# Three mixture-of-experts stages: rows stored in token order and gathered by slot tile, with the order of some instructions changed in two attention stages

## Chip, core and metric

The kernel runs on one core of a Trainium2 chip. Its time is the device time of one execution in microseconds (us); the median of three runs of the kernel before is 4051.39 us (4050.05 to 4054.77).

## What is computed

The reference carries x of shape (128, 32, 128), 4096 tokens of 128 channels in float32, through twelve sublayers: four times cross-attention (to 257 context tokens, or, in the second, causal over the first 32), a self-attention or a retention, and a feed-forward stage. Each reads a layernorm of x and is added to it. Cut to the three mixtures and the two kinds of stage that the change touches:

```python
# L0 ffn: mixture, top 2 of 8 experts, plus a shared expert (a_moe)
probs = softmax(normed @ router_w.T); top_v, top_i = top_k(probs, 2); gates = softmax(top_v)
out = sum_e comb[:, e] * swiglu(normed, gate_up_w[e], down_w[e]) + swiglu(normed, shared...)
# L1 ffn: mixture, top 2 of 8, gelu, at most 1280 tokens for an expert (c_moe)
# L3 ffn: rmsnorm, top 1 of 8, u1 * sigmoid(u2), biases (u_moe)
# L0 attn: six layers of linear attention and a leaky feed-forward part (the stage "l")
# L0, L2, L3 xattn: att = softmax(q k / sqrt(8)); y = (att v) Wo, 16 heads, 257 keys
```

## The kernel before, in words

x lies in on-chip memory as X[128 partitions, 32 tiles, 128 channels], a tile being 128 tokens; four tiles are a chunk, and there are eight chunks. Stages follow one another as blocks. In a block every engine (TensorE, VectorE, ScalarE, GpSimd, SyncE) has its own instruction stream in an order written out by hand; they meet in semaphores alone. In what follows, a stage's name is the prefix of its tiles in the profile: a_cross, l, a_moe, c_self, c_moe, e_cross, retention, q_ffn, t_cross, t_self, t_mlp, u_self, u_moe.

**The mixtures** (`routed_experts`, line 1345) have a head and a loop over slot tiles. In the head VectorE takes the statistics of the chunks (`statistics`, L1736), GpSimd makes factor and shift of each chunk out of small operations with the power function (`deviation`, L1458), ScalarE normalises (`apply`, L1649), TensorE transposes the rows and multiplies them by the router (`turn`, `choose`, L1517 and L1525). The tokens are taken in two halves, g = 0 and 1. For each, VectorE picks the experts (`choose`, L1751), TensorE counts tokens of each expert with two triangular or all-one matrices (L1544), and VectorE works out for each token the slot in which it belongs (`places`, L1772), and for each slot tile the expert that owns it (owner). A slot tile is 128 slots of one expert; a half has 39 slot tiles with two experts for each token (K = 2, in a_moe and c_moe) and 24 with one (K = 1, u_moe), each in 13 or 8 triples. Then GpSimd scatters: `put(g)` (L1482) issues an indirect DMA for each token tile and k, 32 or 16 for a half, which writes 128 normalised rows to their slots in DRAM (L1491). Only when the scatter of a half is complete may SyncE load its triples (`load`, L1427, L1433). Because a slot that no token fills is still computed on, the stage l writes zeros over the slots once: GpSimd sets `blank` and SyncE issues six DMAs of it (L2889). In c_moe VectorE also ranks the tokens of each expert before the loop, to drop those over the capacity (L1814 to L1834).

**The loop over slot tiles** has 78 steps (48 with K = 1). TensorE transposes the tile (`turn_x`, L1587), multiplies it by the owner's first matrix (`up`), transposes the hidden layer (`turn_hidden`), multiplies by the second (`down`); ScalarE and VectorE carry results on; SyncE stores a triple of results back into the slots (L1439). Beside it GpSimd scatters the second half (`put(1)`), and then gathers results: `take(g)` (L1494, L1502), 32 or 16 indirect DMAs for a half, each adding to a tile of X when VectorE combines it (`combine`, L1899, from step 45 on, or 30 with K = 1).

**The stage l** (`linear_transformer`, line 2780) runs 48 chunk steps (six layers of eight chunks) as a software pipeline: in one step TensorE works on chunk `now`, on the attention of the one before (`one`), and on the feed-forward part of the ones before that (`two`, `three`). Its order (L3070 to L3112) puts four bursts of small 32x32 products (`attend`, L3035, 16 products each, one for each tile of the chunk) between the large products `up(two, 2)`, `down(two, 0)` and `up(two, 3)`. GpSimd's order (L2940 to L2954) is: deviation, bias, queries' softmax, deviation and `apply1` for the following chunk, `units` (L2930), and last `leaky(two, 2)` and `leaky(two, 3)` (L2936), for which TensorE's `down(three, 2)` and `down(three, 3)` wait in the next step. ScalarE's `raw(two, 2)` comes ahead of the copy that carries the attention on (L3169 to L3172).

**The cross-attentions** (`cross_attention`; three stages of 128 steps, a batch each): TensorE makes `scores` (L2309) in four banks, VectorE takes the negated maxima in two halves of two banks (`maximum`, L2497), then adds the bias to the next batch's keys (`keys`, L2511), ScalarE takes four exponentials (L2454), the first two after the first half, the others after the second. TensorE's `turn(n - 2, 1)` (L2367) waits for `keys`, since both use the same bank, then come `values` (L2377) and the next `scores`, which also wait for all four exponentials.

## Time and profile before

| what | value |
|---|---|
| median of three runs | 4051.39 us |
| profiled execution, its own time | 4054.11 us |
| its span on the core | 4052.3 us |
| busy of the span: TensorE, VectorE, ScalarE, GpSimd | 85%, 65%, 57%, 61% |
| instructions | 120030 |
| mean granted TensorE clock | 0.92 of full speed |

How to read it: the span runs from the first to the last instruction; what the execution's own time has beyond it lies around the kernel. Busy shares are averages over stages with different limits, so a stage is read by itself: its window, then its timeline. Times in a row are microseconds from the span's start, then the duration; PE is TensorE, PEld its weight load, DVE VectorE, ACT ScalarE, POOL GpSimd. A bracket at a row's end is the idle time before it and what ended it.

### The profile page before, as it was taken

The numbers are of one execution on the slowest core, as the hardware profiler recorded it, in microseconds if no ns is written. First come the engines' busy times: TensorE is split into PE (matmuls) and PEld (weight loads), VectorE is DVE, ScalarE is ACT, GpSimd is POOL, SyncE is SP. The second block draws the span as 40 slices with busy tenths as digits, with TensorE's granted clock in tenths as the row PEclk, the third lists the DMA queues.
The fourth block names the chain that finished last, engine by engine and source line by source line (L and its number), as shares of the span: only waits on it lengthen the run. The fifth ranks groups of instructions, "written<-read, shape, count | busy, mean of one in ns | idle before, by whom it ended". The sixth has DMA issues, their size and how long they took to land. (4 is left out here: it accounts for less than half of the span.)

```text
span 4052.3 us, 120030 instructions
## 1 busy us (share of the span) xinstructions
PE 3461.1 (85%) x44674; PEld 2487.3 (61%) x44674; DVE 2627.4 (65%) x6958; ACT 2325.4 (57%) x6315; POOL 2470.0 (61%) x2844
## 2 busy tenths in 40 slices
PE   8999959999999669698498999978589999786866
PEld 6777737777777447455366777755367777453444
DVE  6777756666666423476434888767767777754655
ACT  6777736666566334287123777755567777544633
POOL 6676656666666543476424887756466766745633
PEclk9999979999999779899699999989599999887978
DMA  2111110000000122201122111110011110000023
GB/s 74 41 35 41 30 69 5 7 11 11 6 7 2 54 63 77 56 17 45 49 72 67 48 47 43 36 65 4 1 47 41 35 41 30 3 2 6 2 91 93
DMA packets 90550, 149.06 MB, mean 37 GB/s; under 512 B 10112, under 2 KB 66816, under 8 KB 89664
## 3 DMA queue, kind: packets, MB, share of 16 engines
q1 hardware_dynamic: 79936, 122.87, 9.8%
q0 software_dynamic: 10240, 20.99, 1.7%
q8 instruction: 261, 4.28, 0.4%
q14 instruction: 113, 0.93, 0.1%
HBM read 112.76 MB, written 31.06 MB: 35 GB/s over the span
## 5 line engine op out<-in xcount | busy, mean ns | idle before, releaser
L2228 POOL TENSOR_TENSOR t_cross_E<-t_cross_E,t_cross_inverse 128x1028 f32<-128x1028 f32 x128 | 243.2, 1900 | 139.7 <-DVE t_cross_inverse L2507 139.7
L2228 POOL TENSOR_TENSOR a_cross_E<-a_cross_E,a_cross_inverse 128x1028 f32<-128x1028 f32 x128 | 243.2, 1900 | 131.9 <-DVE a_cross_inverse L2507 131.9
L2454 ACT ACTIVATE t_cross_E<-t_cross_psum,t_cross_negtop 128x257 f32<-128x257 f32 x512 | 235.9, 474 | 134.6 <-DVE t_cross_negtop L2497 134.6
L2454 ACT ACTIVATE a_cross_E<-a_cross_psum,a_cross_negtop 128x257 f32<-128x257 f32 x512 | 236.0, 474 | 125.8 <-DVE a_cross_negtop L2497 125.8
L2454 ACT ACTIVATE e_cross_E<-e_cross_psum,e_cross_negtop 128x257 f32<-128x257 f32 x512 | 235.9, 474 | 124.2 <-DVE e_cross_negtop L2497 124.2
L2228 POOL TENSOR_TENSOR e_cross_E<-e_cross_E,e_cross_inverse 128x1028 f32<-128x1028 f32 x128 | 243.1, 1899 | 92.7 <-DVE e_cross_inverse L2507 92.7
L3065 PE MATMUL l_psum<-l_ffn_w,l_hidden 128*128 128x128 f32 x1536 | 219.5, 287 | 12.9 <-POOL l_hidden L2938 9.8
L3065 PEld LDWEIGHTS l_psum<-l_ffn_w,l_hidden 128*128 128x128 f32 x1536 | 192.1, 193 | 50.3 <-POOL l_hidden L2938 24.0
L3058 PE MATMUL l_psum<-l_hT,l_ffn_w 128*128 128x512 f32 x384 | 204.3, 635 | 0.9 <-ACT l_hT L3122 0.9
L2497 DVE TENSOR_REDUCE t_cross_negtop<-t_cross_psum 128x2 f32<-128x514 f32 x256 | 165.1, 687 | 47.7 <-PE t_cross_psum L2314 45.9
L2497 DVE TENSOR_REDUCE a_cross_negtop<-a_cross_psum 128x2 f32<-128x514 f32 x256 | 165.1, 686 | 40.3 <-PE a_cross_psum L2309 37.8
L2497 DVE TENSOR_REDUCE e_cross_negtop<-e_cross_psum 128x2 f32<-128x514 f32 x256 | 165.1, 687 | 36.9 <-PE e_cross_psum L2309 32.6
L2367 PE MATMUL a_cross_psum<-const_sb,a_cross_E 128*128 128x128 f32 x1024 | 161.1, 280 | 14.2 <-DVE a_cross_kT L2511 11.5
L2367 PE MATMUL e_cross_psum<-const_sb,e_cross_E 128*128 128x128 f32 x1024 | 160.5, 280 | 14.3 <-DVE e_cross_kT L2511 11.6
L2367 PE MATMUL t_cross_psum<-const_sb,t_cross_E 128*128 128x128 f32 x1024 | 160.9, 280 | 13.5 <-DVE t_cross_kT L2511 11.6
L2917 POOL TENSOR_SCALAR l_normed<-inner,l_moments,l_rstd 128x128 f32<-128x128 f32 x192 | 149.8, 793 | 14.8 <-POOL l_rstd L2911 14.8
L2928 POOL TENSOR_TENSOR l_q<-l_q,l_q_stat 128x512 f32<-128x512 f32 x48 | 50.8, 1058 | 173.0 <-DVE l_q_stat L3201 173.0
L3221 DVE TENSOR_TENSOR inner<-l_psum,inner 128x512 f32<-128x512 f32 x48 | 33.2, 692 | 184.6 <-PE l_psum L3050 184.6
L3042 PEld LDWEIGHTS l_psum<-l_qT,l_ctx 32*32 32x32 f32 x6144 | 65.6, 107 | 114.1 <-issue 108.5
L2367 PEld LDWEIGHTS a_cross_psum<-const_sb,a_cross_E 128*128 128x128 f32 x1024 | 114.8, 142 | 32.9 <-DVE a_cross_kT L2511 30.6
L2367 PEld LDWEIGHTS e_cross_psum<-const_sb,e_cross_E 128*128 128x128 f32 x1024 | 114.1, 141 | 33.1 <-DVE e_cross_kT L2511 31.0
L2938 POOL TENSOR_TENSOR l_hidden<-l_hidden,l_less 128x512 f32<-128x512 f32 x96 | 123.0, 1302 | 18.3 <-ACT l_hidden L3146 18.3
(754 smaller groups left out, 11137.2 us busy)
## 6 DMA issues: line engine op xcount, KB each, us to landing
a_cross_context<-context SPq DMA_DIRECT2D x32, 578.0 KB, 3.7
e_cross_context<-context SPq DMA_DIRECT2D x32, 578.0 KB, 3.7
t_cross_context<-context SPq DMA_DIRECT2D x32, 578.0 KB, 3.7
u_moe_weights<-pack_u_moe SPq DMA_DIRECT2D x1, 5633.0 KB, 16.7
slots<-l_blank SPq DMA_DIRECT2D x6, 832.0 KB, 12.0
a_moe_x_slots<-slots SPq DMA_DIRECT2D x26, 192.0 KB, 2.8
slots<-a_moe_y_slots SPq DMA_DIRECT2D x26, 192.0 KB, 2.0
c_moe_x_slots<-slots SPq DMA_DIRECT2D x26, 192.0 KB, 2.9
```

What stands on the lines that cost most here:

```text
L2228: pool.tensor_tensor(E[:, n % N], E[:, n % N], spread(inverse[:, n % 4], SK, 2), ALU.mult).then_inc(s_unit, 1)
L2367: last = pe.transpose(psum[:, (T_BANK, K_BANK)[c], g * P:(g + 1) * P], E[:, n % N, g, c * P:(c + 1) * P], ident)
L2454: act.activation(E[:, n % N, g], psum[:, g, 0:SK], ACT.Exp, bias=negtop[:, n % 2, g:g + 1], accum_out=total[:, n % 2, g:g + 1]).then_inc(s ...
L2497: dve.tensor_reduce(negtop[:, n % 2, at], psum[:, at, 0:SK], AX.X, ALU.max, negate=True).then_inc(s_top, 1)
L2917: last = pool.tensor_scalar(Y1[:, t], c.tile(t), moments[:, 0, t, 0:1], rstd[:, 0, 1, t:t + 1], ALU.subtract, ALU.mult)
L2928: pool.tensor_tensor(groups, groups, spread(q_stat[:, 2], DH, 2), ALU.mult).then_inc(s_soft, 1)
L2938: pool.tensor_tensor(hidden[:, f], hidden[:, f], less[:, f - 2], ALU.add).then_inc(s_late, 1)
L3042: last = pe.matmul(psum[rows, C_BANK, b * S:(b + 1) * S], ctx[rows, b], qT[rows, b * S:(b + 1) * S], start=True, stop=True)
L3058: pe.matmul(psum[:, U_BANKS[f % 2]], c.ffn(f * P), hT2[:], start=True, stop=True).then_inc(s_up, 1)
L3065: last = pe.matmul(psum[:, D_BANK, t * P:(t + 1) * P], hidden[:, f, t * P:(t + 1) * P], c.ffn((NF + f) * P), start=(f == 0 and t == 0), st ...
L3221: dve.tensor_tensor(c.chunk(), tiles(psum[:, C_BANK]), c.chunk(), ALU.add).then_inc(s_mid, 1)
```

## The change

1. Mixtures. Normalised rows are stored by SyncE in token order in DRAM (`rows`), eight plain DMAs. `place` (slot of a token) is split into slot tile and spot in it. For each pair m of token tile and k, VectorE or GpSimd makes a 128x128 matrix that holds the token's number where its spot is, and TensorE multiplies it by the one-hot matrix of the token's slot tile; the sum over the 32 (or 16) pairs is, for each slot, the number of its token. GpSimd then gathers each slot tile (x_slots) by one indirect DMA with 128 of these numbers. The scatter, `put` and the plain loads are gone, and with them the blanks in l. Results are gathered as before, but in the loop by turns with the slot tiles' gathers.
2. Heads of the mixtures. The norm's factor comes from a square root on ScalarE and a reciprocal on VectorE instead of GpSimd; VectorE applies it to chunks 1 and 3; all statistics come ahead of the first choice.
3. c_moe. The ranking is cut into 18 parts, one at every second step of the loop, from step 2 to step 36.
4. l. TensorE's four bursts `attend` stand together; GpSimd's two `leaky` stand ahead of `units`; ScalarE's `raw(two, 2)` stands behind the copy of the attention.
5. Cross-attentions. VectorE's `keys` stand between the two halves of `maximum`.

```diff
@@ routed_experts, SyncE @@
-            def load(j):
-                g, at = divmod(j, TRIPLES)
-                if at == 0:
-                    sp.wait_ge(s_put[g], puts + 16 * HALF * K)
...
+            def store_rows(c):
...
+                sp.dma_start(slots.rows[c * CHUNK:(c + 1) * CHUNK].rearrange("(t p) d -> p t d", p=P),
+                             rows[:, c * TPC:(c + 1) * TPC]).then_inc(s_rows[c // PART], 16)
@@ GpSimd @@
-            for c in range(PART + 2):
-                deviation(c)
-            put(0)
-            put(1)
+            def index(g):
+                h = of(g)
+                pool.wait_ge(s_spot, g + 1)
+                for n, m in enumerate(BY_POOL):
...
+                    pool.tensor_scalar(at_spot_pool[:, (g * len(BY_POOL) + n) % POOL_RING], core.const("count"), spot[:, k, at:at + 1],
+                                       core.const("token")[:, at:at + 1], ALU.is_equal, ALU.mult).then_inc(s_at_spot_pool, 1)
+            def load(i):
+                j, n = divmod(i, 3)
+                g, at = divmod(i, NS)
+                if at == 0:
+                    pool.wait_ge(s_token, g + 1)
...
+                if n == 0 and j >= 4:
+                    pool.wait_ge(s_x_turn, j - 3)
+                pool.indirect_dma_start(x_slots[:, j % 4, n], None, slots.rows,
+                                        bass.IndirectOffsetOnAxis(ap=token[:, g, at:at + 1], axis=0)).then_inc(s_load[j % 4], 16)
...
+            for g in range(2):
+                index(g)
+            for i in range(NS + AHEAD):
+                load(i)
+            stores_done(pool, TRIPLES)
+            for i in range(NS + AHEAD, COUNT):
+                if i - NS - AHEAD < PAIRS:
+                    take(i - NS - AHEAD)
+                load(i)
@@ TensorE @@
+            def find(g):
+                pe.wait_ge(s_in_tile, g + 1)
+                for m in range(PAIRS):
...
+                    pe.matmul(psum[:, COUNT_BANK + g, FOUND], mine, in_tile[:, k, t], start=m == 0, stop=m == PAIRS - 1).then_inc(s_found, 1)
...
+                if g == 1:
+                    find(0)
                 pe.wait_ge(s_mask, g + 1)
...
+            find(1)
@@ ScalarE @@
+                    act.activation(root[:, at], first, ACT.Sqrt, bias=core.const(eps)[:, 0:1]).then_inc(s_root, 1)
@@ VectorE @@
+                link(dve.tensor_scalar(tile_no[:, 0:K, h], place[:, 0:K, h], 1.0 / P, 0.5 / P - 0.5, ALU.mult, ALU.add))
...
+                dve.tensor_tensor(in_tile[:], spread(tile_no[:, 0:K, h], NS, 3),
+                                  spread(spread(core.const("count")[:, 0:NS], HALF, 1), K, 1), ALU.is_equal).then_inc(s_in_tile, 1)
...
+            def index(g):
+                dve.wait_ge(s_spot, g + 1)
+                for n, m in enumerate(BY_DVE):
...
+                    if n >= RING:
+                        dve.wait_ge(s_found, g * PAIRS + BY_DVE[n - RING] + 1)
+                    dve.tensor_scalar(at_spot[:, n % RING], core.const("count"), spot[:, k, at:at + 1],
+                                      core.const("token")[:, at:at + 1], ALU.is_equal, ALU.mult).then_inc(s_at_spot, 1)
+                dve.wait_ge(s_found, (g + 1) * PAIRS)
+                dve.tensor_copy(token[:, g], psum[:, COUNT_BANK + g, FOUND]).then_inc(s_token, 1)
...
+            for g in range(2):
+                choose(g)
+                places(g)
+                index(g)
@@ loop of VectorE @@
+                if choice == "capacity" and 2 <= i < 38 and i % 2 == 0:
+                    rank((i - 2) // 18, (i - 2) // 2 % 9)
@@ cross_attention, VectorE @@
                 if exists(i, n):
-                    maximum(i, n)
+                    maximum(i, n, 0)
                 if exists(i, n + 1):
                     keys(i, n + 1)
+                if exists(i, n):
+                    maximum(i, n, 1)
@@ linear_transformer, GpSimd @@
-                if now.exists:
-                    units(now)
                 if two.exists:
                     leaky(two, 2)
                     leaky(two, 3)
+                if now.exists:
+                    units(now)
@@ linear_transformer, TensorE @@
                 if one.exists:
-                    attend(one, 0)
+                    for t in range(TPC):
+                        attend(one, t)
                 if two.exists:
                     up(two, 2)
-                if one.exists:
-                    attend(one, 1)
-                if two.exists:
                     down(two, 0)
-                if one.exists:
-                    attend(one, 2)
-                if two.exists:
                     up(two, 3)
-                if one.exists:
-                    attend(one, 3)
-                if two.exists:
                     down(two, 1)
```

Of the pairs m, every fifth (m = 4, 9, ...) is made by GpSimd in a ring of four matrices, the others by VectorE in a ring of eight; a matrix may be overwritten once its product is done.

## Rows read from the trace of the kernel before

**Rows 1.** Stretches: length, then busy time of PE, PEld, DVE, ACT, POOL, granted clock, DMA share, GB/s
```profile
545.00:1373.00 828.00, 790.39 (x11616) 587.23 (x11616) 535.83 (x1586) 479.64 (x816) 544.24 (x625) 0.98 0.02 6
1373.00:1462.00 89.00, 23.70 (x105) 22.08 (x106) 31.74 (x146) 19.46 (x43) 58.35 (x104) 0.51 0.22 84
1462.00:1657.00 195.00, 190.66 (x1093) 146.90 (x1094) 67.35 (x188) 92.37 (x183) 60.86 (x64) 0.99 0.25 72
3876.00:3927.00 51.00, 22.56 (x104) 21.15 (x105) 25.60 (x128) 15.54 (x40) 25.41 (x32) 0.54 0.38 149
```

**Rows 2.** Timeline of l, one step: start, duration, engine, line, operation
```profile
810.27 1.02 PE L3015 MATMUL l_psum<-l_hT,l_attn_w 128*128 128x512 f32 x2
...
811.13 1.05 PE L3065 MATMUL l_psum<-l_ffn_w,l_hidden 128*128 128x128 f32 x8
...
816.38 0.45 PE L3042 MATMUL l_psum<-l_qT,l_ctx 32*32 32x32 f32 x32
...
816.76 1.13 PE L3058 MATMUL l_psum<-l_hT,l_ffn_w 128*128 128x512 f32 x2
...
817.81 0.46 PE L3042 MATMUL l_psum<-l_qT,l_ctx 32*32 32x32 f32 x32
...
822.67 2.50 POOL L2938 TENSOR_TENSOR l_hidden<-l_hidden,l_less 128x512 f32<-128x512 f32 x2
...
827.85 1.11 DVE L3228 TENSOR_SCALAR l_normed<-inner,l_moments,l_rstd 128x128 f32<-128x128 f32 x4
...
832.93 0.45 PE L3042 MATMUL l_psum<-l_qT,l_ctx 32*32 32x32 f32 x32
```

**Rows 3.** Waits in l, 545 to 1373 us: in total, times, longest
```profile
PEld l_psum L3065 <- POOL l_hidden L2938: 24.0, 47, 3.0
```

**Rows 4.** Timeline, start of l on GpSimd
```profile
515.87 1.49 POOL L2901 MEMSET l_blank<- 128x1664 f32 x1 [6.75 <-POOLq L167]
```

**Rows 5.** Timeline of a_cross, one step, TensorE, VectorE and ScalarE
```profile
312.25 0.71 PE L2309 MATMUL a_cross_psum<-a_cross_kT,a_cross_q_heads 32*128 32x257 f32 x8
...
313.04 1.29 DVE L2497 TENSOR_REDUCE a_cross_negtop<-a_cross_psum 128x2 f32<-128x514 f32 x2 [0.77 <-PE a_cross_psum L2309]
...
314.25 0.47 DVE L2511 TENSOR_SCALAR a_cross_kT<-a_cross_psum,a_cross_weights 128x257 f32<-128x257 f32 x1
...
315.49 0.21 ACT L2454 ACTIVATION_READ_ACCUMULATOR a_cross_E<-a_cross_psum,a_cross_negtop 128x1 f32 x1
...
315.94 0.72 PE L2309 MATMUL a_cross_psum<-a_cross_kT,a_cross_q_heads 32*128 32x257 f32 x8
```

**Rows 6.** Timeline, head of a_moe
```profile
1396.73 0.29 DVE L1734 TENSOR_TENSOR a_moe_l<-a_moe_psum,a_moe_router 128x128 f32<-128x128 f32 x1 [16.41 <-PE a_moe_psum L1530]
...
1403.59 1.22 PE L1544 MATMUL a_moe_psum<-a_moe_p,const_sb 128*128 128x128 f32 x4 [6.97 <-DVEq L1770]
...
1409.48 1.22 POOL L1491 DMA_INDIRECT slots<-inner,a_moe_place_i  x1 [10.96 <-DVE a_moe_place_i L1791]
...
1461.94 0.90 PE L1592 MATMUL a_moe_psum<-const_sb,a_moe_x_slots 128*128 128x128 f32 x3 [9.95 <-DMA a_moe_x_slots<-slots]
```

**Rows 7.** Timeline, head of c_moe
```profile
1907.85 0.87 DVE L1739 BATCH_NORM_STATS2 c_moe_stats<-X 128x6 f32<-128x128 f32 x4 [0.32 <-PEq L167]
...
1909.06 0.84 DVE L1739 BATCH_NORM_STATS2 c_moe_stats<-X 128x6 f32<-128x128 f32 x4
...
1912.96 1.09 PE L1522 MATMUL c_moe_psum<-const_sb,hT_all 128*128 128x128 f32 x4 [6.15 <-ACT hT_all L1653]
...
1915.51 1.72 PE L1530 MATMUL c_moe_psum<-c_moe_router,c_moe_fT 128*128 128x8 f32 x8
...
1924.30 0.29 DVE L1734 TENSOR_TENSOR c_moe_l<-c_moe_psum,c_moe_router 128x128 f32<-128x128 f32 x1 [9.31 <-PE c_moe_psum L1530]
...
1991.55 0.88 PE L1592 MATMUL c_moe_psum<-const_sb,c_moe_x_slots 128*128 128x128 f32 x3 [16.92 <-issue]
```

**Rows 8.** Timeline, gathers of results behind a_moe's loop
```profile
1660.75 0.94 POOL L1502 DMA_INDIRECT a_moe_got<-slots,a_moe_place_i  x1 [0.30 <-issue]
```

More of the change, by code:

```diff
@@ L1328, in __init__ @@
     def __init__(self, ctx, nc, tiles):
+        self.rows = nc.dram_tensor("rows", [TOK, P], F32, kind="Internal").ap()
         self.halves = [nc.dram_tensor(f"slots{g}", [tiles * P, P], F32, kind="Internal").ap() for g in range(2)]
-        self.s_put = [ctx.enter_context(nc.semaphore(f"put{g}")) for g in range(2)], 0
+        self.s_load = [ctx.enter_context(nc.semaphore(f"load{n}")) for n in range(4)], [0] * 4
         self.s_got = [ctx.enter_context(nc.semaphore(f"got{n}")) for n in range(4)], 0
@@ L1440, in store @@
                              ).then_inc(s_store[j % 3], 16)
-            for j in range(4):
-                load(j)
+            for c in range(CHUNKS):
+                store_rows(c)
             for j in range(2 * TRIPLES):
-                if j + 4 < 2 * TRIPLES:
-                    load(j + 4)
                 store(j)
@@ L1511, in _ @@
+            stores_done(pool, TRIPLES)
[3 more added lines that the diff above has]
+                load(i)
+            for n in range(COUNT - NS - AHEAD, PAIRS):
+                take(n)
+            stores_done(pool, 2 * TRIPLES)
             if not behind:
-                take(1)
-            pool.wait_ge(s_put[1], puts + 16 * HALF * K)
+                for n in range(PAIRS, 2 * PAIRS):
+                    take(n)
@@ L1749, in statistics, with factors, apply @@
                     dve.tensor_tensor(square[:, at], square[:, at], moments[:, at, 1], ALU.add).then_inc(s_square, 1)
+            def factors(u):
+                at = slice(2 * u * TPC, 2 * (u + 1) * TPC)
+                dve.wait_ge(s_root, u + 1)
+                if rms:
+                    dve.reciprocal(factor[:, at], root[:, at]).then_inc(s_factor, 1)
+                else:
+                    dve.reciprocal(factor[:, at], root[:, at]).then_inc(s_inverse, 1)
+                    dve.wait_ge(s_inverse, u + 1)
+                    dve.scalar_tensor_tensor(out=shift[:, at], in0=moments[:, at, 0], scalar=-1.0, in1=factor[:, at],
+                                             op0=ALU.mult, op1=ALU.mult).then_inc(s_factor, 1)
+            def apply(c):
+                dve.wait_ge(s_factor, c // 2 + 1)
+                for at in range(c * TPC, (c + 1) * TPC):
+                    if rms:
+                        last = dve.tensor_scalar(rows[:, at], source[:, at], factor[:, at:at + 1], None, ALU.mult)
+                    else:
+                        last = dve.tensor_scalar(rows[:, at], source[:, at], factor[:, at:at + 1], shift[:, at:at + 1],
+                                                 ALU.mult, ALU.add)
+                last.then_inc(s_normed, 1)
             def choose(g):
@@ L1942, in routed_experts @@
         sc.close_block()
-        slots.s_put, slots.s_got = (s_put, puts + 16 * HALF * K), (s_got, gots + 16 * FETCHED * K // 4)
+        slots.s_got = s_got, gots + 16 * FETCHED * K // 4
+        slots.s_load = s_load, [loads[n] + 48 * len(range(n, 2 * TRIPLES, 4)) for n in range(4)]
 def mlp(core, name, w, base):
@@ L2777, with linear_transformer @@
 ATTN_WIDTH, FFN_WIDTH = 5 * P + 2, 8 * P + 2
-def linear_transformer(core, name, stream, slots):
+def linear_transformer(core, name, stream):
     nc, X = core.nc, core.X
@@ L2884, in _ @@
                 sp.dma_start(ffn_w[:, side], ffn_dram[:, side * FFN_WIDTH:(side + 1) * FFN_WIDTH]).then_inc(s_ffn_w[side], 16)
-            sp.wait_ge(s_blank, 1)
-            for lot in slots:
-                for third in range(3):
-                    rows = lot[third * blank.shape[1]:(third + 1) * blank.shape[1]]
-                    sp.dma_start(rows.rearrange("(p r) c -> p (r c)", p=P), blank[:]).then_inc(s_slots, 16)
             with sp.Fori(1, DEPTH // 2) as i:
@@ L3168, in step @@
                     values_out(now, one)
-                if two.exists:
-                    raw(two, 2)
                 if one.exists:
@@ L3173, in step @@
                 if two.exists:
+                    raw(two, 2)
                     raw(two, 3)
```

211 lines of the change are left out of this document (116 added, 95 removed).

## The prediction

> **What bounds the kernel now.** I cut the span into stages and read the busy time of each window first, then the timelines, then the waits. In l, TensorE is busy 790 of 828 us at a granted clock of 0.98, the upper of its two levels (2.4 GHz) [rows 1]: a gain there must come out of TensorE's own stream, or out of the 38 us in which it stands still. One wait holds 24.0 of those: 47 times TensorE waits for GpSimd's leaky (L2938) [rows 3]. In a_moe's loop TensorE is busy 191 of 195 us, VectorE 67, GpSimd 61 [rows 1], so nothing moved into the loop on these two should show. The head ahead of it is the reverse: 89 us with TensorE busy 24, at a granted clock of 0.51 (1.2 GHz), GpSimd 58 [rows 1]. The scatter lies there: from its first DMA to the first transpose of the loop are 1461.94 - 1409.48 = 52.5 us [rows 6]. In the cross-attentions two chains turn in step, which their timeline shows: scores, the two maxima, keys, TensorE's turn, values, scores; and scores, maxima, four exponentials, scores. A step is 3.69 us from scores to scores [rows 5], and there are 3 x 128.
>
> **Change 4, l.** A step is 16.55 us from first `attend` to first `attend` [rows 2]. A large product behind a burst of small ones takes 1.05 us to the next instruction (816.76 to 817.81); one of the same shape (128x512, two passes) between large ones takes 0.86 (810.27 to 811.13) [rows 2]. So each change between large and small costs 0.19, and three round trips go: 0.57. A burst from its start to the next product is 0.38 [rows 2]; how much of it is filling and draining no row shows, between 0 and, say, half. I take 0.1 for each of three, 0.3. Together 0.87 a step. The `leaky` pair now comes ahead of `units`, so the wait of 24.0 us over 47 steps (0.51) goes. That makes 1.38 of 16.55, leaving 15.2 on TensorE; but a chain through GpSimd, VectorE and TensorE that carries the layer along turns nearly as fast, and I can read no single row for it. GpSimd is busy 544 of 828 us [rows 1], so it isn't that engine alone. I let the chain hold the step at 15.5 and take 1.04 x 48 = **50 us**. Bounds: 20 (only the leaky wait goes) and 66 (all 1.38). What is late next: `units` itself, 2.5 us of leaky later than now [rows 2], needed only when the context is masked. ScalarE's `raw(two, 2)` behind the copy costs nothing: its consumer, leaky, has slack, and if that is gone the rest of the leaky wait returns. The blanks: GpSimd's memset of 1.49 us stands first in l, ahead of what the first step needs [rows 4]; gain 1.4. Its six DMAs run under l.
>
> **Change 5, cross.** The two maxima take 1.29 together, 0.65 each; keys 0.47 [rows 5]. After the change keys end 0.65 earlier and the second maximum 0.47 later, unless the next bank of scores comes no sooner anyway. The chain by keys loses up to 0.65; the chain by the exponentials ends at 315.70, 0.24 before the next scores [rows 5], so it is next in line. Its first two exponentials don't wait for the second maximum, and hide part of the 0.47. I take 0.03 a step, **12 us** in 384; bounds 0.1 better (38) and 0.1 worse (-38).
>
> **Changes 1 to 3, head of a_moe**, step by step from 1373.2. Statistics of four chunks, 1.21 each [rows 7], 4.8; factors (two small VectorE operations) and ScalarE's apply, about 2.4 by the same path in c_moe (first statistics to first turn 5.1, of which 1.2 statistics [rows 7], so 3.9 with GpSimd's powers in it); so first turn at 7.2. From first turn to first logits in c_moe 11.3 [rows 7]: 18.5, where 23.5 stands now. To the mask 6.9 (1396.73 to 1403.59 [rows 6]), counting and the second half's turns and router products 12: 37.5. Now find(0), 32 products. Four router products of two passes each take 1.72 at the lower clock [rows 7], 0.43 each: 13.8 at that clock, 6.9 at twice it. I take 9, since both levels are possible in an engine that has just become busy. VectorE makes 26 matrices in 0.28 each, 1.11 for four [rows 2], 7.2, beside it, GpSimd six. Choosing again 6.9, counting and places 5.9 (to 1409.48 [rows 6]): 59.3. New on VectorE: four operations on 128x32 at 0.2, in_tile of 1248 elements at the rate of a maximum (0.65 for 514 [rows 5]) 1.6, the owners about 1.5, now ahead of the first matrix: 63.3. find(1) again 9 to 10: 73. GpSimd's first gathers come out about then: three at 0.94 + 0.30 [rows 8] and their landing; 75. The head is 88.7 now: **13.7**, bounds 5 (both finds at the lower clock, later gathers) and 20. The eight stores of rows (256 KB each) run beside it on SyncE.
>
> **c_moe's head** is 83.7 now [rows 7], as GpSimd's chain is short there; the same working without softmax, plus the rank products that stand between find(1) and the loop, gives 75: **9**, bounds 3 and 15. The ranking itself is hidden in both kernels, by the scatter now, and in 18 pieces by VectorE's idle time in the loop (128 of 195 us in a_moe's, [rows 1]) after. **u_moe's head** is 51 [rows 1], with 16 pairs a half. There statistics come 3 us later (the square adds to four chunks), two finds at 5 and four in_tile operations are new, against 16 scatter DMAs of 1.25, that partly ran beside: 54, **-3**, bounds -8 and +3.
>
> **Loops.** GpSimd issues 39 + 12 gathers ahead, then 27 pairs of take and load, 2.48 a pair at 1.24 each [rows 8], against 195/78 = 2.5 a tile [rows 1]: nothing, but with no room. Takes behind the loop stay as they are.
>
> A rule speaks against this: by the Trainium skill (SBUF — State Buffer, "SBUF: two separate sides") VectorE in a mode that uses both port pairs shuts GpSimd out, and GpSimd can't write a DMA's descriptors meanwhile; loads that SyncE issued are now GpSimd's. The rows of the gathers behind the loop, 0.94 each beside VectorE's combining [rows 8], don't show it; were each gather held up for one VectorE operation, the loops would be the third rival's.
>
> **Sum**: 50 + 1.4 + 12 + 13.7 + 9 - 3 = 83. The profiled execution's own time is 4054.11, the median 4051.39; from the median, 3968, rounded 3969.
>
> **Rivals.**
> 1. The bursts cost what their columns cost, and grouping gives nothing; the chain through GpSimd holds l. For it: 0.19 is read from one step. l gives 22 and the time is 3997. 15%.
> 2. The second maximum is late for the exponentials, 0.1 a step: for it, only 0.24 us of room against up to 0.47 [rows 5]. 50 us worse than the sum: 4019. 10%.
> 3. Slower than before: the price of a gather on GpSimd. Place: the loops, where each tile needs one and pairs need two. At price g for a load the K = 2 loops are long by 78 (g - 2.5) + 27 x 1.24 once g is over 2.5: the gain of 83 is gone at 2.6; at 3.0 each loses 72, and the time is 3968 + 145 = 4113. Against it: 1.24 for the same kind of DMA [rows 8]. 4%.
> 4. The change doesn't do what it says: the two finds with their chains of VectorE work take as long as the scatter did. Then the mixtures give nothing, 3989. 8%.
>
> The forecast has the other 63%.
>
> **How the numbers follow.** About 0.2%, 8 us, can be told from no change. The forecast's own spread is l's and the heads' bounds, 3935 to 3990; rivals 1 and 4 lie at its edge, 2 outside. The range 3935 to 4015 leaves out rival 3, most of 2 and a little below. Only rival 3, or 2 together with 1, comes near 4043: faster 0.93, same 0.03, slower 0.04.
>
> **What would show it.** Right: in l, four attends in one row of about 1.2 to 1.5 us, steps of 15.3 to 15.7, the wait for L2938 under 5 us; heads of about 75, 75 and 54, with find's products between the logits and the loop; loops of 195 still. Wrong: TensorE in the loop waiting for x_slots, or find's products at over 0.5 us; cross steps at 3.8; l at over 16.

## The result and the profile after

The kernel after takes 4018.62 us (median of 4, 4014.49 to 4023.05) against 4053.08 of the kernel before (4 runs): 0.9916 of it, 95% interval 0.9898 to 0.9933. The direction was forecast, the size was not: 34.5 us, where the sum said 83, and the time lies 4 us above the top of the range (4015). The profiled execution spans 4014.7 us, 37.6 less than before's 4052.3. By stages, each from its first instruction to that of the next (SyncE's, which runs ahead, left aside):

| stage | before | after | gain | forecast |
|---|---|---|---|---|
| l | 857.3 | 823.0 | 34.3 | 50 + 1.4 |
| three cross-attentions | 1535.0 | 1526.6 | 8.4 (t_cross 7.6) | 12 |
| a_moe | 334.1 | 326.6 | 7.5 | 13.7 |
| c_moe | 292.0 | 292.5 | -0.5 | 9 |
| u_moe | 175.7 | 190.4 | -14.7 | -3 |

The rest differs by 2.6 us in all. So the orders moved in l and in the cross-attentions are more than the whole gain, and the rewritten mixtures together lose 7.7 us. First the stretches of the kernel after, for [rows 1]: length, busy time of PE, PEld, DVE, ACT, POOL, granted clock, DMA share, GB/s.

```profile
514.00:1336.00 822.00, 749.37 (x11616) 579.04 (x11616) 569.72 (x1689) 475.18 (x816) 558.22 (x647) 0.97 0.03 8
1337.00:1420.00 83.00, 50.61 (x232) 49.19 (x232) 56.62 (x227) 19.71 (x41) 21.34 (x21) 0.51 0.26 91
1420.00:1616.00 196.00, 191.70 (x1092) 147.31 (x1092) 67.04 (x187) 92.38 (x183) 96.07 (x102) 0.98 0.25 61
1864.00:1943.00 79.00, 53.67 (x240) 51.94 (x241) 53.62 (x216) 17.72 (x39) 21.83 (x22) 0.51 0.26 87
3824.00:3881.00 57.00, 37.08 (x168) 35.61 (x168) 36.56 (x178) 15.39 (x37) 10.68 (x12) 0.50 0.41 143
```

a_moe's loop is as it was, TensorE 192 of 196 us and GpSimd now at 96 instead of 61. The head has changed character: TensorE is busy 51 of 83 us, where it was 24 of 89, still at a granted clock of 0.51, the lower level. Now one step of l, for [rows 2] (timeline: start, duration, engine, line, operation; in brackets the idle time before it and what ended it).

```profile
809.37 3.12 POOL L3008 TENSOR_SCALAR l_normed<-inner,l_moments,l_rstd 128x128 f32<-128x128 f32 x4 [0.31 <-POOL l_rstd L3002]
812.46 2.50 POOL L3029 TENSOR_TENSOR l_hidden<-l_hidden,l_less 128x512 f32<-128x512 f32 x2
813.78 1.16 PE L3156 MATMUL l_psum<-l_ffn_w,l_hidden 128*128 128x128 f32 x8 [0.26 <-POOL l_hidden L3029]
...
820.00 1.08 PE L3122 MATMUL l_psum<-l_v_own,l_k_tok 128*32 128x128 f32 x32
...
822.12 0.86 DVE L3293 BATCH_NORM_STATS2 l_stats<-inner 128x6 f32<-128x128 f32 x4
822.92 1.29 PE L3133 MATMUL l_psum<-l_qT,l_ctx 32*32 32x32 f32 x128
823.14 0.38 DVE L3297 BATCH_NORM_AGGREGATE l_moments<-l_stats 128x2 f32<-128x6 f32 x4 [0.15 <-DVE l_stats L3293]
823.60 0.20 POOL L3000 TENSOR_TENSOR l_rstd<-l_moments,const_sb 128x4 f32<-128x4 f32 x1 [0.80 <-DVE l_moments L3297]
...
825.20 3.12 POOL L3008 TENSOR_SCALAR l_normed<-inner,l_moments,l_rstd 128x128 f32<-128x128 f32 x4 [0.31 <-POOL l_rstd L3002]
828.29 2.49 POOL L3029 TENSOR_TENSOR l_hidden<-l_hidden,l_less 128x512 f32<-128x512 f32 x2
829.62 1.16 PE L3156 MATMUL l_psum<-l_ffn_w,l_hidden 128*128 128x128 f32 x8 [0.38 <-POOL l_hidden L3029]
```

The four bursts are one row of 1.29, as forecast. But from leaky to leaky it is 15.83 us, and TensorE still stands 0.26 to 0.38 us ahead of `down(three, 2)`. The chain is to be read upwards: leaky stands right behind apply1 (3.12), that behind the deviation, that behind VectorE's statistics (822.12 to 823.52), those, through VectorE's masking of the context, behind TensorE's products of L3122, and those behind the leaky of the step before. The wait of [rows 3] has not gone. That row is of the weight loads (PEld), which run beside the products. From 545 to 1330 us it is now 26.3 us in 43 times, and TensorE's products themselves (PE) wait 16.1 us:

```profile
PEld l_psum L3156 <- POOL l_hidden L3029: 26.3, 43, 1.0
PE l_psum L3156 <- POOL l_hidden L3029: 16.1, 42, 0.8
```

In the kernel before, the products' own row (545 to 1373 us) was well under the 24.0 of the loads:

```profile
PE l_psum L3065 <- POOL l_hidden L2938: 9.8, 19, 2.8
```

### The profile page after: what moved, and what is told of

The parts are those of the page before. It is cut to its first block and busy times, and to the rows that moved or that the text cites. A ratio compares the mean times of both kernels' runs of the same rounds, so it can differ in the third digit from the quotient of the medians.

```text
span 4014.7 us, 120813 instructions
## 1 busy us (share of the span) xinstructions
PE 3462.6 (86%) x44994; PEld 2541.7 (63%) x44994; DVE 2722.1 (68%) x7168; ACT 2360.6 (59%) x6308; POOL 2491.8 (62%) x2797
## 5 line engine op out<-in xcount | busy, mean ns | idle before, releaser
L3156 PE MATMUL l_psum<-l_ffn_w,l_hidden 128*128 128x128 f32 x1536 | 207.6, 278 | 18.9 <-POOL l_hidden L3029 18.1
L2595 DVE TENSOR_REDUCE t_cross_negtop<-t_cross_psum 128x2 f32<-128x514 f32 x256 | 175.8, 687 | 33.4 <-PE t_cross_psum L2412 31.9
L2595 DVE TENSOR_REDUCE a_cross_negtop<-a_cross_psum 128x2 f32<-128x514 f32 x256 | 175.4, 686 | 26.7 <-PE a_cross_psum L2407 26.3
L2595 DVE TENSOR_REDUCE e_cross_negtop<-e_cross_psum 128x2 f32<-128x514 f32 x256 | 175.6, 686 | 25.3 <-PE e_cross_psum L2407 25.2
L3008 POOL TENSOR_SCALAR l_normed<-inner,l_moments,l_rstd 128x128 f32<-128x128 f32 x192 | 149.8, 794 | 14.8 <-POOL l_rstd L3002 14.8
L2465 PEld LDWEIGHTS t_cross_psum<-const_sb,t_cross_E 128*128 128x128 f32 x1024 | 121.3, 142 | 0.9 <-ACT t_cross_ET L2542 0.4
```

What stands on the lines that cost most here:

```text
L2465: last = pe.transpose(psum[:, (T_BANK, K_BANK)[c], g * P:(g + 1) * P], E[:, n % N, g, c * P:(c + 1) * P], ident)
L2595: dve.tensor_reduce(negtop[:, n % 2, at], psum[:, at, 0:SK], AX.X, ALU.max, negate=True).then_inc(s_top, 1)
L3008: last = pool.tensor_scalar(Y1[:, t], c.tile(t), moments[:, 0, t, 0:1], rstd[:, 0, 1, t:t + 1], ALU.subtract, ALU.mult)
L3156: last = pe.matmul(psum[:, D_BANK, t * P:(t + 1) * P], hidden[:, f, t * P:(t + 1) * P], c.ffn((NF + f) * P), start=(f == 0 and t == 0), st ...
```

## Experiments

Differences are read by stage, as above, from one profile of each kernel. How far a stage differs by itself can be seen where its code is the same: l is 820.7 us in after_ring and 827.8 in after_again, and 854.9 in cross_only against 857.3 before; a_cross is 505.8 in after and 507.9 in orders_only.

Four chips were used. On two of them the mixtures' loops of every kernel with the new mixtures took 18 to 33 us longer each. One of them ran after_drain, after_base, after_warm and after_ring: 4086.65, 4094.78, 4085.18 and 4085.25 us, one run each, where the kernel before took 4072.92 there in one run. So on that chip the kernels with the new mixtures were 12 to 22 us slower than the kernel before, in spite of the orders' gain in l. The other ran best_warm. These runs are read by their heads and ends, and not by their whole times.

### l: one order alone, and the other alone

```diff
# l_attends, on the kernel before, TensorE
-                    attend(one, 0)
...
+                    for t in range(TPC):
+                        attend(one, t)
```

> The kernel before with one edit: in l, TensorE's four bursts attend stand together. Stage l took 855.6 us before and 821.2 after the whole change, a step from one attend to the next 16.4 on the mean before and 15.8 after. Theory (grouping saves the filling and draining of the array, 1.22 for the four in one against 4 x 0.38): l shorter by 20 to 35 us, unless the chain through GpSimd's leaky holds it; with leaky still behind units, the wait of TensorE for leaky then grows above 24 us and l is shorter by 15 to 25. Rival (the bursts cost what they cost, the whole gain of l comes from GpSimd's order): l shorter by less than 5 us, and the wait for leaky unchanged at about 24.

```diff
# l_leaky, on the kernel before, GpSimd
-                if now.exists:
-                    units(now)
                 if two.exists:
                     leaky(two, 2)
                     leaky(two, 3)
+                if now.exists:
+                    units(now)
```

> The kernel before with one edit: in l, GpSimd's two leaky stand ahead of units. Theory: the wait of TensorE for L2938 (24.0 us in 47 times) nearly goes and l is shorter by 10 to 24 us, since TensorE is otherwise full. Rival (leaky was held by apply1 and by ScalarE's raw ahead of it, units is not what held it, or units is now late for own context): l shorter by less than 5 us, and a new wait appears on VectorE for unit.

The stage l took 852.5 us with the attends alone (4.8 less, and only 2.4 less than in cross_only, so hardly clear of the spread), 845.6 with leaky alone (11.7 less, inside theory's 10 to 24), 823.0 with both: 34.3, twice the sum. (The kernel after also has ScalarE's `raw(two, 2)` behind the copy, which no run took by itself, so a part of the 34.3 can be its.) The whole was 4050.58 and 4038.87 us, one run each, against 4051.26. The waits of l_attends for leaky say why (in total, times, longest):

```profile
PEld l_psum L3065 <- POOL l_hidden L2938: 52.5, 42, 1.8
PE l_psum L3065 <- POOL l_hidden L2938: 42.5, 42, 1.6
```

The window is 545 to 1330 us; on TensorE's products that wait was 6.2 us in the same window of the kernel before. Grouping does free the time: 42.5 - 6.2 = 36 us go into the wait and 5 into the stage, 0.86 a step, as in the sum (0.87). Most steps of l_attends take 16.27 us, the turn of the chain through GpSimd with `units` in it. With leaky alone TensorE no longer waits for it (no such row in its waits from 545 to 1330 us), and most steps take 16.15: its own stream with four bursts is the bound left, which is argued from the missing wait. Neither edit is worth its price without the other. Theory had 15 to 25 us for the attends. The rival, under 5 us, was met in the number, but not in its reason: the wait grew, as theory said.

### l: is it the chain through apply1?

```diff
# after_tile, on the kernel after
# GpSimd's apply1
-                for t in range(TPC):
+                for t in range(TPC - 1):
...
# VectorE, last in its step
+                if following.exists:
+                    apply1(following)
...
# TensorE's turn1 and GpSimd's add_bias
                 pe.wait_ge(s_norm1, c.before + 1)
+                pe.wait_ge(s_norm1d, c.before + 1)
```

VectorE's `apply1` normalises the fourth tile.

> The kernel after with one edit: in l, VectorE normalises the fourth tile of each chunk for apply1, GpSimd the first three. Theory (a chain TensorE, VectorE statistics, GpSimd deviation and apply1, leaky, TensorE holds the step at 15.8, and TensorE waits 0.3 to 0.4 for leaky in each): GpSimd's leaky starts 0.78 earlier, the waits of TensorE for L3029 (42 us, PE and its loads together) go to under 10, and l is shorter by 12 to 20 us. Rival (TensorE's own stream is the bound and the waits only fill gaps that it has anyway): l within 4 us of 821.

l took 802.4 us, 20.6 less than in after, just above theory's 12 to 20; the whole 4002.72 us in one run. Of the wait for leaky this is left (545 to 1310 us):

```profile
PEld l_psum L3160 <- POOL l_hidden L3031: 0.8, 2, 0.5
PE l_psum L3160 <- POOL l_hidden L3031: 0.3, 1, 0.3
```

So the chain held the step. From first attend to last, 47 steps, the mean step was 16.49 us before, 15.81 in after and 15.36 in after_tile, so TensorE's own stream is at 15.36 or below. l_leaky, where the wait is gone too but the four bursts stand apart, has 16.27 on the mean, 0.91 more.

### The cross-attentions alone

```diff
# cross_only, on the kernel before, VectorE
                 if exists(i, n):
-                    maximum(i, n)
+                    maximum(i, n, 0)
                 if exists(i, n + 1):
                     keys(i, n + 1)
+                if exists(i, n):
+                    maximum(i, n, 1)
```

> The kernel before with one edit: in the cross-attentions VectorE's keys stand between the two halves of maximum. Theory A (the second maximum comes later and holds the third exponential; the steps without a pick lose what the steps with one gain): a_cross and e_cross within 3 us of before, t_cross shorter by 6 to 9, the whole 3 to 10 us faster. Theory B (the edit is good everywhere, and something else of the change took it back in a_cross and e_cross): 15 us or more faster.

4043.46 us against 4051.26, ratio 0.9983, interval 0.9974 to 0.9993: theory A. a_cross was 1.4 us longer, e_cross 0.2, t_cross 8.2 shorter. A step of the kernel after, for [rows 5] (timeline of a_cross):

```profile
311.39 0.72 PE L2407 MATMUL a_cross_psum<-a_cross_kT,a_cross_q_heads 32*128 32x257 f32 x8
312.17 0.69 DVE L2595 TENSOR_REDUCE a_cross_negtop<-a_cross_psum 128x2 f32<-128x514 f32 x1 [0.62 <-PE a_cross_psum L2407]
312.95 0.49 DVE L2609 TENSOR_SCALAR a_cross_kT<-a_cross_psum,a_cross_weights 128x257 f32<-128x257 f32 x1
313.35 0.68 DVE L2595 TENSOR_REDUCE a_cross_negtop<-a_cross_psum 128x2 f32<-128x514 f32 x1
313.36 0.47 ACT L2552 ACTIVATE a_cross_E<-a_cross_psum,a_cross_negtop 128x257 f32<-128x257 f32 x1
314.07 0.48 ACT L2552 ACTIVATE a_cross_E<-a_cross_psum,a_cross_negtop 128x257 f32<-128x257 f32 x1
315.18 0.31 PEld L2407 LDWEIGHTS a_cross_psum<-a_cross_kT,a_cross_q_heads 32*128 32x128 f32 x8 [0.20 <-ACT a_cross_E L2552]
```

The second exponential is done at 313.83, the second maximum at 314.03, and the third exponential starts behind it at 314.07: a quarter of a microsecond lost, and at the end the scores wait 0.20 for the exponentials. That is the second rival's mechanism, at work. A normal step went from 3.69 to 3.76 us (mean of 3.75, 3.79, 3.72 in a_cross), and the step with a pick, every fourth, from about 4.2 to 4.0, since keys are out ahead of it there. In a_cross and e_cross the two cancel within the spread (in after they are 1.1 shorter and 0.3 longer); in t_cross, whose normal steps were 3.77 before, only the gain is left. With the orders of l and the crosses together and the mixtures as before:

> The kernel before with the change's parts 4 and 5 alone (the orders in l and in the cross-attentions), the mixtures as before. Theory (by stages, the whole gain of the change is in l and t_cross, 34 and 8 us; the mixtures sum to nothing on one chip and to a loss on the chip of the last four runs, where the loops of every variant of after took 20 to 30 us longer from the first result gather on): 38 to 46 us faster than before on any chip, so as fast as after or faster. Rival (the mixtures' part gains too, and the orders are worth less without it): less than 30 us faster.

4012.24 us against 4049.72, ratio 0.9908, interval 0.9893 to 0.9923, where the kernel after on the same chip took

> The kernel after, unchanged, on the chip of this call. Theory (the mixtures' loops depend on how soon stores and gathers land, which differs from chip to chip): either 34 us faster than before with loops of 182, 187 and 88 us, or, on a chip like the last, within 15 us of before or slower with loops over 200, 205 and 100. Rival (what was slow in the last four runs was their edits): 34 us faster in both cases.

4020.46 us, ratio 0.9931, interval 0.9917 to 0.9944. So 37.5 us for the orders alone, just under theory's 38 to 46, and 29 for the whole change, with loops of 181, 189 and 88 us, nearly as short as in after (theory's first case, which had 34). The mixtures' part is worth -8 us there, as the stage table says.

### The heads of the mixtures

The head of the kernel after, a_moe, in one place of each kind: find(0)'s first eight (timeline, for [rows 6]), the tokens taken off, find(1), GpSimd's first gather and the loop.

```profile
1373.34 1.91 PE L1551 MATMUL a_moe_psum<-a_moe_in_tile,a_moe_at_spot 128*128 128x39 f32 x8
...
1387.23 0.20 DVE L1878 CAST a_moe_token<-a_moe_psum 128x39 int32<-128x39 f32 x1 [3.92 <-PE a_moe_psum L1551]
...
1403.78 1.90 PE L1551 MATMUL a_moe_psum<-a_moe_in_tile,a_moe_at_spot 128*128 128x39 f32 x8 [8.36 <-DVE a_moe_at_spot L1875]
...
1409.38 1.22 POOL L1492 DMA_INDIRECT a_moe_x_slots<-rows,a_moe_token  x1 [0.19 <-issue]
...
1420.61 0.87 PE L1614 MATMUL a_moe_psum<-const_sb,a_moe_x_slots 128*128 128x128 f32 x3 [2.98 <-issue]
```

Five products follow one another in 2.13 us (1373.34 to the next row of its kind at 1375.47), 0.43 each, so each find takes 13.8 us (1373.3 to 1387.2, 1403.8 to 1417.6). The steps of the sum fit to find(0): first logits at 17.5 us (18.5 forecast), find(0) from 35.6 (37.5). Then each find took 13.8, the bound, instead of 9, and the head 82.8 instead of 75. Two experiments look at it.

```diff
# after_warm, on the kernel after, TensorE
                 last.then_inc(s_count, 1)
+            for n in range(10 if K == 2 else 7):
+                pe.matmul(psum[:, 7], core.const("ident"), core.const_sb[:, 0:512], start=True, stop=True)
             find(1)
```

> The kernel after with one edit: between counting and find(1) TensorE makes 10 products of 128x512 (7 in u_moe) that nothing reads, into a bank that is free. In after TensorE stands still there for 8.4 us in a_moe, and find(0) and find(1) take 13.8 us each, 0.43 for a product, at the lower granted clock. Theory (the clock is low because TensorE had little to do, and would rise under dense work): find(1) takes 7 to 8 us in a_moe and c_moe, 3.5 to 4.5 in u_moe, and each head is shorter by 3 to 6 us. Rival (small products as find's are held at 0.43 by something else than the clock, weight loads or the semaphores of VectorE): find(1) stays at 13.8 and the whole the same or up to 3 us longer.

The same place in after_warm (timeline; the first row is of the added products):

```profile
1398.73 6.99 PE L1568 MATMUL a_moe_psum<-const_sb 128*128 128x512 f32 x15
1405.56 0.98 PE L1551 MATMUL a_moe_psum<-a_moe_in_tile,a_moe_at_spot 128*128 128x39 f32 x8
...
1408.83 1.08 PE L1551 MATMUL a_moe_psum<-a_moe_in_tile,a_moe_at_spot 128*128 128x39 f32 x8
...
1410.14 1.91 PE L1551 MATMUL a_moe_psum<-a_moe_in_tile,a_moe_at_spot 128*128 128x39 f32 x8
```

It is the clock: the same eight passes take 0.98 us behind the dense products, and 1.91 again 4.6 us later. The stretches say so too (columns as in [rows 1]; the granted clock is 0.96, then 0.50, and 0.50 through both finds of after):

```profile
1405.60:1410.10 4.50, 4.50 (x41) 4.50 (x40) 4.19 (x16) 0.00 (x0) 2.75 (x3) 0.96 0.00 0
1410.20:1415.40 5.20, 5.20 (x25) 5.11 (x24) 0.87 (x4) 0.00 (x0) 3.85 (x5) 0.50 0.19 52
```

find(1) took 9.9, 10.4 and 3.7 us, where it had taken 13.8, 13.8 and 7.0 (theory had 7 to 8 for the first two); it began 2 us late, behind the added products, so the heads gained 1.6, 1.5 and 1.3 us, less than theory's 3 to 6. In a_moe the loop did not take that over: its second triple of slot tiles took 16.4 us, where it is 8.2, 8.5 and 9.6 in after_drain, after_base and after_ring on the same chip.

```diff
# after_ring, on the kernel after, VectorE
-    RING, POOL_RING, AHEAD = 8, 4, 12
+    RING, POOL_RING, AHEAD = len(BY_DVE), 4, 12
...
-            for g in range(2):
-                choose(g)
-                places(g)
-                index(g)
+            choose(0)
+            places(0)
+            index(0)
+            choose(1)
+            found(0)
+            places(1)
+            index(1)
+            found(1)
```

`found` is the end of `index`, the wait for the products and the copy of the tokens.

> The kernel after with one edit: VectorE's ring of at_spot holds all 26 (13) matrices of a half, and VectorE makes choose(1) between making them and taking the tokens of find(0) off. In after VectorE sits in the ring's waits until find(0) ends at 1387.2, though the second logits are there at 1373. Theory (find(0) is on the path only because VectorE waits in it): the heads of a_moe and c_moe are shorter by 5 to 7 us each, u_moe's by 1 to 2, together 11 to 16. Rival (TensorE's find(0) would be slowed by matrices that come later, or the head is then held by GpSimd's matrices or the gathers): less than 4 us in all.

Heads of 75.6, 73.0 and 55.2 us where after has 82.8, 79.2 and 57.6: 15.8 in all, theory's upper end (of c_moe's 6.2, 0.9 was won ahead of find(0), as in after_drain, which has no such edit). VectorE had the second half's logits 14 us before find(0) was over (TensorE's last router product lies right ahead of 1373.3), and sat in the ring's waits: the sum had counted find(0) as a term in a row, and it was that only through VectorE's order.

### c_moe's end

The kernel after, between the last result and the next stage (timeline):

```profile
2144.58 0.29 DVE L1992 COPY c_moe_y_slots<-c_moe_psum 128x128 f32<-128x128 f32 x1 [1.35 <-PE c_moe_psum L1645]
2144.89 0.36 SPq L1455 DMA_DIRECT2D slots<-c_moe_y_slots  x1
...
2156.47 0.31 POOL L2363 MEMSET e_cross_last_of<- 128x256 f32 x1 [24.24 <-POOLq L169]
2156.50 0.29 DVE L2576 BATCH_NORM_STATS2 e_cross_stats<-X 128x6 f32<-128x128 f32 x1 [11.63 <-PEq L169]
```

11.63 us in which no engine computes; in the trace's records GpSimd's last instruction of the block, a drain with which the block closes, takes 9.04 of them, from 2147.18 on. In the kernel before it took 8.90, but from 2183.7 on, beside the last steps of the loop, and the gap was 2.55. The change put a wait for all stores ahead of it, which only the takes of the second half need, and in c_moe these are in the next block.

```diff
# after_drain, on the kernel after, GpSimd
-            stores_done(pool, 2 * TRIPLES)
             if not behind:
+                stores_done(pool, 2 * TRIPLES)
```

> The kernel after with one edit: in c_moe, whose second half of results is gathered in the next stage, GpSimd no longer waits for the last store before it leaves the block. In after, 11.6 us pass between c_moe's last VectorE operation and e_cross's first, 9.0 of them GpSimd's closing of its block, which starts only when that wait ends; before it was 2.5. Theory (the closing takes 9 us behind indirect DMAs whenever it starts, and the new wait puts it behind the last store): the gap is 2.5 to 3 us again, the whole 9 us shorter. Rival (the closing waits for the stores, or for something else that ends at 2156): the gap stays above 10 us.

```profile
2206.61 0.29 DVE L1992 COPY c_moe_y_slots<-c_moe_psum 128x128 f32<-128x128 f32 x1 [1.35 <-PE c_moe_psum L1645]
...
2209.46 0.29 DVE L2576 BATCH_NORM_STATS2 e_cross_stats<-X 128x6 f32<-128x128 f32 x1 [2.56 <-PEq L169]
```

The gap is 2.56 again: 9.1 us. The drain itself takes 10.22 us there, from 2193.10 on, beside the loop.

### u_moe's base

In the kernel after, at the start of u_moe's loop (timeline):

```profile
3880.49 4.42 DVE L1932 TENSOR_TENSOR X<-X,inner 128x4096 f32<-128x4096 f32 x1
3880.88 4.85 POOL L1492 DMA_INDIRECT u_moe_x_slots<-rows,u_moe_token  x1 [0.30 <-issue]
3886.04 0.94 POOL L1492 DMA_INDIRECT u_moe_x_slots<-rows,u_moe_token  x1 [0.31 <-issue]
```

One gather takes 4.85 us instead of 0.94, and ends 0.8 us behind VectorE's addition, beside which it was issued; it is 4.80 to 4.85 in each of the six profiles that have the addition there. Before, the addition stood in the same place, but SyncE issued the loads. By the Trainium skill (SBUF — State Buffer, "SBUF: two separate sides") a VectorE operation with two inputs in on-chip memory holds the ports that it shares with GpSimd for its whole length, against a GpSimd operation that reads on-chip memory. The trace agrees, if a gather, which takes its 128 numbers from on-chip memory, counts as one. The prediction named the section's other rule, on VectorE's two-port modes, and weighed it against rows in which VectorE's operations were 0.35 us long and the gathers 0.94.

```diff
# after_base, on the kernel after, VectorE, ahead of choose(0)
             factors(2)
             factors(3)
+            if base is not None:
+                dve.tensor_tensor(X[:], X[:], base[:], ALU.add).then_inc(s_base, 1)
+                dve.wait_ge(s_base, 1)
...
# and away from its place behind the owners
-            if base is not None:
-                dve.tensor_tensor(X[:], X[:], base[:], ALU.add).then_inc(s_base, 1)
-                dve.wait_ge(s_base, 1)
```

> The kernel after with one edit: u_moe's addition of its base to X (4.42 us on VectorE, 128x4096, both inputs in on-chip memory) stands ahead of the first choice, where VectorE waits 3.5 us for logits, instead of beside GpSimd's gathers. Theory (one gather took 4.85 us instead of 0.94 because VectorE's long operation kept GpSimd from issuing it, and TensorE then waited for x_slots): the gather is 0.94, the waits of TensorE for x_slots (4.5 us) go, and u_moe is 2 to 4 us shorter, of which up to 1 us is given back in the head. Rival (the long gather is a matter of its own, as a full queue): it stays long in the same place, u_moe no shorter.

The tile's instructions in after_base, and then in after (duration in ns, least, median, most):

```profile
L1492 POOL DMA_INDIRECT u_moe_x_slots<-rows,u_moe_token x48: 938/944/1112, 3933.4 to 4037.7; - x48
```

```profile
L1492 POOL DMA_INDIRECT u_moe_x_slots<-rows,u_moe_token x48: 940/944/4848, 3874.5 to 3966.4; - x48
```

The long gather is gone, and the head 0.8 us longer. What it is worth in the loop could not be read there; in best, below, u_moe's loop is 85.6 us instead of 88.2, 84.2 before.

### Four edits together, and a fifth

> The kernel after with four edits together: VectorE normalises the fourth tile in l; GpSimd leaves c_moe's block without the last wait; u_moe's base is added ahead of the choice; a ring of all matrices, with choose(1) ahead of taking off find(0). Theory (they lie in different stretches and add up: 20 in l, 9 at c_moe's end, 2 to 4 in u_moe's loop, 14 to 16 in the heads): 45 to 50 us faster than after, 80 to 85 faster than before on a chip where after gains 34. Rival (loops or ends give part back, as the shorter head leaves GpSimd's gathers no lead): 30 us or less faster than after.

3975.44 us (5 runs) against 4049.72, ratio 0.9817, interval 0.9804 to 0.9831; 45 us faster than after_again beside it, 37 faster than orders_only. Against after_again theory holds, at its lower end; against before it is 74 and not 80 to 85, as after itself gained 29 there and not 34. By stage: l 801.9, a_moe 317.6, c_moe 278.1, u_moe 184.4. So a_moe and c_moe are 16.5 and 13.9 us shorter than before, and on this chip the new mixtures do pay; u_moe alone stays 8.7 longer, where only 16 scatters of 1.25 us a half went, and two finds with their matrices came.

> The kernel best with one more edit: 8 products of 128x512 (5 in u_moe) that nothing reads stand ahead of find(1). In after_warm 10 (7) of them made find(1)'s products 0.22 instead of 0.43, for the first 4 us of it in a_moe and for all of it in u_moe, but find(1) also began 2 us late. Theory (fewer of them end in time and still raise the clock): find(1) begins within 1 us of best's and takes 9 to 11 us in a_moe and c_moe, 4 in u_moe; each head 2 to 4 us shorter than best's 75.6, 73.8 and 56.0; 7 to 10 us in all, less where GpSimd's gathers are what the loop waits for. Rival (8 are too few to raise it, or the gathers hold the head): heads within 1 us of best's.

The edit is after_warm's with 8 (5) products, on top of best. find(1) began within 1 us of best's and took 9.5, 10.5 and 4.2 us; the heads are 71.3, 69.7 and 53.9, 4.3, 4.1 and 2.1 shorter than best's (of the 4.1, 0.9 was won ahead of find(1)). Theory, with 10.5 in all, as far as the heads go. But the whole took 4050.75 us against 4059.43 there (ratio 0.9978, 0.9967 to 0.9988): a_moe's, c_moe's and u_moe's loops took 214.0, 216.4 and 108.2 us, 181.1, 186.7 and 85.6 in best. In a_moe the second triple took 16.8 us (7.7 in best, 9.6 in after_ring on the other chip with long loops), as in after_warm; more than the head's 4.3. No run has these products on a chip with short loops, so what they are worth to the whole is not shown.

## Why the prediction was wrong

**What bounds.** Right for the loops and the heads, and for which wait to look at in l. For l it named a chain through GpSimd as nearly as fast as TensorE, and had no row for it. It took the 24.0 us of [rows 3], a row of weight loads that run beside the products, for time in which TensorE stands still; the products' own row is 9.8.

**Change 4.** The step that failed is "I let the chain hold the step at 15.5". It holds it at 15.81 on the mean: 0.68 a step instead of 1.04, and 34 us in l instead of 50 (l_attends, l_leaky, after_tile). The 16.55 from which it took off was one step, the mean was 16.49. Of the two terms, grouping was near (0.86 to 0.91 a step for 0.87), and the leaky wait was put at 0.51, more than twice what it measured: by itself its end gave 0.22 a step, 11.7 us (l_leaky). Taking 0.86 and 0.22 from 16.49 leaves 15.41, near the 15.36 of after_tile, where the sum had 15.2. That the wait "goes" once `units` is behind it was right by itself and wrong beside the grouping. The chain could have been read: [rows 2] end leaky at 825.17, and apply1 ahead of units was in the same timeline. The blanks' 1.4 us can't be seen in the spread of l: it is 821.4 in orders_only, which has them, and 823.0 in after.

**Change 5.** The 0.03 a step came out as 8.4 / 384 = 0.02, but not by its reason. The normal steps lost 0.07, as the second rival had it (0.1), and the pick steps, which the sum left out, gave 0.2 back.

**The heads.** Everything up to find(0) was within 2 us. The step that failed is "I take 9, since both levels are possible": both finds ran at 0.43 a product, the bound, 13.8 (heads of 82.8, 79.2 and 57.6 for 75, 75 and 54: each in its bounds, near the poor end). after_warm shows that the other level is there to be had.

**Missing from the sum**: the 9.1 us at c_moe's end, a wait that the change adds on GpSimd, which the prediction never named (after_drain); u_moe's gather beside the base, 2.6 us of loop in best; and 3.5 us behind u_moe's loop (from its last transpose to the end 44.6 us, 41.1 before), for which no run looked; in the traces the second half's first gather, which waits for the last store, comes 14.8 us behind that transpose, 12.7 before. In c_moe 4 us of shorter loop (186.7 for 190.8), not forecast either, and a_moe's block closing 3 us sooner, stand against them.

**Rivals.** The first had l at 22, and 3997: l gave 34, and l_attends shows its premise false, since grouping frees time. The second is true as a mechanism, a step of a_cross 0.07 longer and not 0.1, but the steps with a pick pay it back. The third, the price of a gather, is not: 0.94 + 0.30 in the loops. Yet what it warned of, loops so long that the kernel is slower than before, is there on one of the chips, with gathers at their old price. The fourth is the nearest to what happened: the mixtures gave nothing, though not because the heads stayed as they were (two are 5.9 and 4.5 us shorter). The 3989 that it named lies 30 too low, by l (17), the crosses (4) and the 8 us that the mixtures lost.

**How the numbers follow.** Each term had its bound, and l, the crosses and the three heads came out within them; but all of them lay on the poor side at once, and one of 9 us had no bound at all. The range did not hold even the terms' own bounds: with l and the three heads at their poor ends (20, 5, 3 and -8) and the crosses and the blanks as forecast, the sum is 33 us and the time 4018, not the 3990 that the prediction gave as the end of its spread. That this 4018 is nearly the time measured is luck, since the 9.1 us at c_moe's end and u_moe's loop and end are not in it.

## What to carry over

Where two nearly equal chains hold a loop, an edit to one shows nothing alone: test them together, and read the step time of each chain from the trace before costing either. A wait added on an engine delays also what its block does last, so its price is to be looked for at the block's end; and a small product on a TensorE that has had little to do is to be costed at the lower clock, as find's 0.43 us here. A wait of the weight loads is not yet a wait of the products. A change that makes many small DMAs is to be measured on more than one chip. When work is moved to GpSimd's DMA queue, look for long VectorE operations beside it.

## What the runs showed of the hardware

- GpSimd's drain at c_moe's end took 9.04 us although the last gather had been issued 15 us before it began; 8.90 in the kernel before and 10.22 in after_drain and best, where it began beside the last gather. It hides only under others' work.
- One indirect DMA issued 0.4 us into a VectorE addition of 128x4096 took 4.85 us; everywhere else they took 0.94 to 1.22.
- In after_warm and best_warm find(1)'s products ran at 0.22 us behind 6 to 11 us of dense ones, and in a_moe and c_moe they fell back to 0.43 after 3.6 to 5.1 us; in a_moe of after_warm the granted clock was 0.96, then 0.50.
- The same kernel's mixture loops took 18 to 33 us longer on two of four chips. In all five runs the triples take what they take on the other chips up to the first gathers of results, but for the first two or three of each loop, and up to 13.5 us from there on, where a_moe has 7.2 on the others. In best_warm VectorE and ScalarE have waits in a_moe's loop whose end the trace puts down to no instruction of this core ("remote"), 32.9 and 18.0 us, rows that best doesn't have:

```profile
DVE a_moe_y_slots L2000 <- remote: 32.9, 8, 5.0
ACT a_moe_hT L1753 <- remote: 18.0, 7, 3.4
```

A gather's issue was 0.94 us in each. The kernel before was profiled on neither chip, so whether its loops suffer as much isn't shown; its times there, 4072.92 (one run) and 4059.43, are 22 and 9 us above the 4050 of the other chips. The cause stays open.
